# Gated delta-rule layer with feed-forward block: the keys decayed to the chunk's end are turned by way of DRAM and VectorE instead of on TensorE

## What is computed

```python
def step(carry, inp):
    S, R = carry
    q_t, k_t, v_t, a_t, aR_t, b_t, g_t = inp
    kn = k_t / jnp.maximum(jnp.linalg.norm(k_t, axis=-1, keepdims=True), 1e-12)
    pred = jnp.einsum('bhji,bhj->bhi', S, kn)
    r = jnp.clip(v_t - pred, -CLIP, CLIP)
    S = a_t[..., None] * S
    kp = jnp.einsum('bhd,bhde->bhe', kn, S)
    S = S + b_t[..., None, None] * kn[..., None] * (v_t - kp)[..., None, :]
    o = jnp.einsum('bhji,bhj->bhi', S, q_t)
    R = aR_t[..., None] * R
    kpR = jnp.einsum('bhd,bhde->bhe', kn, R)
    R = R + g_t[..., None, None] * kn[..., None] * (r - kpR)[..., None, :]
    o = o + jnp.einsum('bhji,bhj->bhi', R, q_t)
    return ((S, R), o)
```

## Time and profile before

| what | value |
|---|---|
| median of 2 runs | 2404.26 us (2404.12 to 2404.41) |
| profiled execution, device time | 2413.72 us |
| its span, first to last instruction | 2411.9 us, mean granted TensorE clock 0.973 |
| TensorE matmuls, weight loads | 2283.6 us (95%), 1927.4 us (80%) |
| VectorE, ScalarE, GpSimd | 1686.8 us (70%), 1240.2 us (51%), 1169.0 us (48%) |
| `turn_kend` (L433) on the chain that ended last | 4% of the span |

### The profile page before, as it was taken

The page is one execution under the profiler, slowest core; times in us unless marked ns, Lnnn a source line. Parts: engine busy times, 40 slices in busy tenths (PEclk is TensorE's granted clock), DMA queues, the critical chain, the costliest instruction groups (busy, mean ns, idle before and its releaser), DMA issues.

```text
span 2411.9 us, 120326 instructions
## 1 busy us (share of the span) xinstructions
PE 2283.6 (95%) x52544; PEld 1927.4 (80%) x52544; DVE 1686.8 (70%) x3725; ACT 1240.2 (51%) x2384; POOL 1169.0 (48%) x2376
## 2 busy tenths in 40 slices
PE   1999996699999999999999999999999999999998
PEld 1544443588999888989888888888888988888887
DVE  6111012778888878888888888888888888888874
ACT  2322232555555555555555555555555555555530
POOL 0000000655666665665565666566665666656641
PEclk8899997789999999999999999999999999999998
DMA  3000000111212121212111212112112122222221
GB/s 89 1 0 0 0 0 20 27 37 37 39 37 42 38 47 36 40 38 40 38 38 38 47 38 40 38 38 38 38 38 49 38 40 42 41 43 41 44 42 25
DMA packets 306094, 84.82 MB, mean 35 GB/s; under 512 B 280368, under 2 KB 302512, under 8 KB 305584
## 3 DMA queue, kind: packets, MB, share of 16 engines
q1 hardware_dynamic: 305584, 77.25, 16.1%
HBM read 41.53 MB, written 35.65 MB: 32 GB/s over the span
## 4 chain that ended last, share of the span: by engine, by line
PE 77%; issue 15%; DMA 2%; DVE 2%; POOL 2%; ACT 1%; SPq 1%; POOLq 0%; ACTq 0%; DVEq 0%
PE bank L453 12%; PE bank L476 5%; PE bank L467 5%; PE bank L433 4%; PE bank L497 3%; PE bank L488 3%; PE bank L415 3%; PE bank L410 3%; PE bank L404 3%; PE bank L553 3%; PE bank L612 3%; PE bank L422 3%; PE bank L395 3%; PE bank L530 3%; PE bank L521 2%
## 5 line engine op out<-in xcount | busy, mean ns | idle before, releaser
L1069 POOL TENSOR_TENSOR lane_t<-lane_n,lane_x 128x15 f32<-128x15 f32 (+7 forms) x960 | 317.6, 331 | 375.7 <-DMA lane_n<-n_dram 305.5
L453 PE MATMUL bank<-kq,Kt 64*64 64x96 f32 x8192 | 363.2, 232 | 1.5 <-issue 0.6
L1072 POOL TENSOR_TENSOR lane_x<-lane_x,lane_t 128x15 f32<-128x15 f32 (+7 forms) x960 | 326.5, 340 | 75.2
L453 PEld LDWEIGHTS bank<-kq,Kt 64*64 64x64 f32 x8192 | 316.8, 135 | 3.5 <-issue 3.4
L1228 ACT ACTIVATE oS<-bank 128x512 f32<-128x512 f32 x64 | 38.2, 597 | 351.4 <-PE bank L601 351.4
L1043 POOL TENSOR_TENSOR KQF<-efull,kn 128x768 f32<-128x768 f32 x64 | 124.6, 1946 | 190.9 <-ACT efull L1183 190.9
L1152 ACT ACTIVATE ea<-bank,nba 128x256 f32<-128x256 f32 x256 | 107.3, 470 | 195.2 <-PE bank L415 140.1
L1205 ACT ACTIVATE kend<-Kt,ek 128x64 f32<-128x64 f32 x768 | 189.8, 340 | 0.0
L1086 POOL MEMSET lane_id<- 128x256 f32 x1 | 0.3, 311 | 389.2 <-DVE acc L758 389.2
L755 DVE TENSOR_TENSOR dn<-bank,s3b 128x512 f32<-128x512 f32 x8 | 5.5, 692 | 239.5 <-PE bank L378 239.5
L849 DVE COPY_PREDICATED AS<-cst,bank 128x384 f32<-128x384 int32 x256 | 143.0, 584 | 31.3 <-PE bank L453 28.6
(11 more groups left out here) (156 smaller groups left out, 6490.9 us busy)
## 6 DMA issues: line engine op xcount, KB each, us to landing
XF<-x_dram SPq DMA_DIRECT2D x256, 64.0 KB, 2.4
lane_n<-n_dram SPq DMA_DIRECT2D x128, 124.0 KB, 2.8
x_dram<-lane_x SPq DMA_DIRECT2D x128, 124.0 KB, 2.3
n_dram<-AS SPq DMA_DIRECT2D x256, 32.0 KB, 2.0
n_dram<-AR SPq DMA_DIRECT2D x256, 32.0 KB, 1.7
wt<-in_win SPq DMA_DIRECT2D x4, 640.0 KB, 4.7
out_y<-acc SPq DMA_DIRECT2D x16, 128.0 KB, 2.0
hw<-in_h1T SPq DMA_DIRECT2D x1, 1024.0 KB, 7.3
```

The costliest lines, as they stand in the source:

```text
L453: ins = pe.matmul(v3(dst[hd[h], o:o + kinds * C], kinds)[:, :, i * SUB:(i + 1) * SUB], Kt[hd[h], m * 96 + i * SUB:m * 96 + i * SUB + C], r ...
L1069: pool.tensor_tensor(tv, lane_n[:, m * SUB + m + 1:m * SUB + BASE].unsqueeze(2).to_broadcast([L, rows, m + 1]), xv[:, m, 0:m + 1].unsqueez ...
L1072: pool.tensor_tensor(xv[:, m + 1:, 0:m + 1], xv[:, m + 1:, 0:m + 1], tv, ALU.subtract).then_inc(s["lane_step"], 1)
```

## The change

`turn_kend` and `copy_kend` are removed, with their semaphores. SyncE writes `kend` to a new DRAM buffer `k_dram` (one DMA of 128 x 3072 bytes) and reads it back into a new SBUF tile `kend_in` with four DMAs of 32 partitions (two runs of 1536 bytes each a partition), so that the halves of the tokens and of the head dimension have changed places between the partition blocks. VectorE then transposes all blocks of 32 x 32 in one instruction of 128 x 768 into `kendT[n % 2]` (two buffers in place of three). `to_end` writes `kend` in the matching order: halves of the tokens outermost. SyncE's new DMAs stand between `lanes_in` and `lanes_out` of the same quad; VectorE's transpose of quad k stands first in its body k. `project_kq` no longer waits for the copy, and `to_end` waits for the DMA out of `kend` instead of for the turning.

```diff
@@ -182,7 +182,8 @@
             KQF = ring("KQF", RING, 5 * 2 * (T - C))
             dec = ring("dec", RING, NM)
             vt = ring("vt", RING, 2 * T)
-            kendT = ring("kendT", 3, 4 * (T - C))
+            kend_in = sbb("kend_in", 4 * (T - C))
+            kendT = ring("kendT", 2, 4 * (T - C))
             AS = ring("AS", 3, NCH * 2 * 3 * C)
             AR = ring("AR", 3, NCH * 2 * 2 * C)
 
@@ -205,6 +206,7 @@
             rS = ring("rS", 2, P)
             oS = sbb("oS", 2 * T)
 
+        k_dram = nc.dram_tensor("k_dram", (2, 4, SUB, 4 * (T - C)), F32).ap()
         n_dram = nc.dram_tensor("n_dram", (2, 4, NM, SUB, SUB), F32).ap()
         x_dram = nc.dram_tensor("x_dram", (2, 4, NM, SUB, SUB), F32).ap()
 
@@ -299,6 +301,20 @@
                     sp.dma_start(lane_n[j * half_lanes:(j + 1) * half_lanes, 0:LANE_RUN],
                                  n_dram[n % 2].rearrange("e m s t -> (e m) (s t)")[:, run]).then_inc(s["n_in"], 16)
 
+            def keys_out(n):
+                need(sp, "kend", n + 1)
+                need(sp, "k_in", (n - 1) * 4 * 16)
+                sp.dma_start(k_dram[n % 2].rearrange("e d t -> (e d) t"), kend[:, :]).then_inc(s["k_out"], 16)
+
+            def keys_in(n):
+                need(sp, "k_out", (n + 1) * 16)
+                need(sp, "kT", n)
+                for h in range(2):
+                    for j in range(2):
+                        e = 2 * h + j
+                        sp.dma_start(v3(kend_in[e * SUB:(e + 1) * SUB, :], 2),
+                                     k_dram[n % 2, 2 * h:2 * h + 2, :, j * 2 * (T - C):(j + 1) * 2 * (T - C)].rearrange("i d t -> d i t")).then_inc(s["k_in"], 16)
+
             def store(n):
                 b = n % B
                 need(sp, "acc_add", n + 1)
@@ -310,6 +326,8 @@
                     blocks_out(k + 2, 0)
                     blocks_out(k + 2, 1)
                     lanes_in(k + 2)
+                    keys_out(k + 2)
+                    keys_in(k + 2)
                     lanes_out(k + 2)
                 if on(k + 5) and (k + 5) % B == 0:
                     load_weights(k + 5)
@@ -388,7 +406,6 @@
 
             def project_kq(n):
                 need(pe, "w_loaded", (n // B + 1) * 16)
-                need(pe, "kT_sb", 2 * (n - 1))
                 need(pe, "kn", n)
                 need(pe, "vt_sb", n)
                 for p in range(2):
@@ -422,17 +439,6 @@
                         ins = pe.matmul(PA1[hd[h], c * P:(c + 1) * P], xh(n)[:, c * C:(c + 1) * C], wt[:, 4 * 256 + h * P:4 * 256 + (h + 1) * P],
                                         start=True, stop=True)
                 ins.then_inc(s["v_ps"], 1)
-
-            def turn_kend(n):
-                need(pe, "kend", n + 1)
-                need(pe, "kn", min(n + 2, NQ))
-                need(pe, "vt_sb", min(n + 2, NQ))
-                for y in range(2):
-                    for m in range(6):
-                        for h in range(2):
-                            ins = pe.matmul((PA0, PA1)[y][hd[h], m * DH:(m + 1) * DH], kend[hd[h], (y * 6 + m) * C:(y * 6 + m + 1) * C],
-                                            ident[hd[h], hd[h]], start=True, stop=True)
-                    ins.then_inc(s["kT_ps"], 1)
 
             def products(n, g):
                 y, chunks = (0, (g,)) if g < NCH else (1, (2 * (g - NCH), 2 * (g - NCH) + 1))
@@ -523,11 +529,11 @@
 
             def s_s(n, c):
                 need(pe, "sy_sb", 4 * n + c + 1)
-                need(pe, "kT_sb", 2 * n + 2)
+                need(pe, "kT", n + 1)
                 for p in range(2):
                     for h in range(2):
                         o = (p * 3 + c) * C
-                        ins = pe.matmul(SB[hd[h], 2 * P + p * DH:2 * P + (p + 1) * DH], kendT[n % 3][hd[h], o:o + C], pc(yS[c % 2], p)[hd[h], :],
+                        ins = pe.matmul(SB[hd[h], 2 * P + p * DH:2 * P + (p + 1) * DH], kendT[n % 2][hd[h], o:o + C], pc(yS[c % 2], p)[hd[h], :],
                                         start=True, stop=True)
                 ins.then_inc(s["ss_ps"], 1)
 
@@ -581,11 +587,11 @@
 
             def r_s(n, c):
                 need(pe, "ry_sb", 4 * n + c + 1)
-                need(pe, "kT_sb", 2 * n + 2)
+                need(pe, "kT", n + 1)
                 for p in range(2):
                     for h in range(2):
                         o = (6 + p * 3 + c) * C
-                        ins = pe.matmul(RB[hd[h], 2 * P + p * DH:2 * P + (p + 1) * DH], kendT[n % 3][hd[h], o:o + C], pc(yR[c % 2], p)[hd[h], :],
+                        ins = pe.matmul(RB[hd[h], 2 * P + p * DH:2 * P + (p + 1) * DH], kendT[n % 2][hd[h], o:o + C], pc(yR[c % 2], p)[hd[h], :],
                                         start=True, stop=True)
                 ins.then_inc(s["rs_ps"], 1)
 
@@ -618,8 +624,6 @@
                 if e:
                     s_p(k - 1, 1)
                     r_s(k - 1, 0)
-                if l:
-                    turn_kend(k + 1)
                 if e:
                     s_w(k - 1, 2)
                     r_w(k - 1, 1)
@@ -871,6 +875,11 @@
                 mask = cst[:, M_Z1:M_Z1 + SUB].bitcast(I32).unsqueeze(1).to_broadcast([P, NM, SUB])
                 dve.copy_predicated(v3(Zf[n % 2][:, :], NM)[:, :, SUB:], mask, v3(IV[:, :], NM)).then_inc(s["z1"], 1)
 
+            def turn_keys(n):
+                need(dve, "k_in", (n + 1) * 4 * 16)
+                need(dve, "rs_ps", 3 * (n - 1))
+                dve.transpose(v4(kendT[n % 2][:, :], 12, 2).rearrange("p m i d -> p i m d"), v4(kend_in[:, :], 2, 12)).then_inc(s["kT"], 1)
+
             def s_right(n, c):
                 need(dve, "sw_ps", 3 * n + c)
                 dve.tensor_tensor(wS[c % 2][:, :], vt[n % RING][:, c * P:(c + 1) * P], SB[:, 0:P], ALU.subtract).then_inc(s["sw_sb"], 1)
@@ -930,6 +939,8 @@
 
             def body(k):
                 a, b, l, d, e, f = on(k + 3), on(k + 2), on(k + 1), on(k), on(k - 1), on(k - 2)
+                if d:
+                    turn_keys(k)
                 if f:
                     s_clip(k - 2, 3)
                 if e:
@@ -1198,19 +1209,13 @@
             def to_end(n):
                 need(act, "kdiag", n + 1)
                 need(act, "kfar", n + 1)
-                need(act, "kT_ps", 2 * n)
+                need(act, "k_out", n * 16)
                 for m in range(4):
                     for c in range(3):
                         o = (m * NCH + c) * 96 + SUB
-                        ins = act.activation(kend[:, (m * 3 + c) * C:(m * 3 + c + 1) * C], Kt[:, o:o + C], ACT.Copy,
+                        ins = act.activation(v4(kend[:, :], 2, 12)[:, :, m * 3 + c], v3(Kt[:, o:o + C], 2), ACT.Copy,
                                              scale=ek[:, 6 * T + m * NCH + c:6 * T + m * NCH + c + 1])
                 ins.then_inc(s["kend"], 1)
-
-            def copy_kend(n):
-                need(act, "rs_ps", 3 * (n - 2))
-                for y in range(2):
-                    need(act, "kT_ps", 2 * n + y + 1)
-                    act.activation(kendT[n % 3][:, y * 2 * (T - C):(y + 1) * 2 * (T - C)], (PA0, PA1)[y][:, 0:2 * (T - C)], ACT.Copy).then_inc(s["kT_sb"], 1)
 
             def level0(n):
                 need(act, "nx0", n + 1)
@@ -1246,8 +1251,6 @@
                 if b:
                     from_anchor(k + 2)
                     gate_inverse(k + 2)
-                if l:
-                    copy_kend(k + 1)
                 if b:
                     to_anchor(k + 2)
                 if a:
```

More of the change, by code:

```diff
@@ L72 @@
     "kk": "k's operands", "kp": "k's operands of the predictions", "qq": "q's operands", "kf": "k against the state", "ea1": "one over S's gate", "kfull": "operands against the state",
-    "kend": "k decayed to the chunk's end", "kT_ps": "turned in PSUM (2)", "kT_sb": "turned in SBUF (2)",
+    "kend": "k decayed to the chunk's end", "k_out": "it is in DRAM", "k_in": "back with its halves of tokens on partitions (4 DMAs)", "kT": "turned",
     "pr_ps": "products in PSUM (6 a quad)", "pr_sb": "masked in SBUF (6 a quad)", "n_sb": "N times beta or gamma (2 a quad)",
```

## The result

The changed kernel took 2441.01 us, median of two runs (2437.09 and 2444.93), against 2404.26: the ratio is 1.0138, 95% interval 1.0074 to 1.0202. Timed again in more rounds it gave 1.0126 of before, interval 1.0104 to 1.0148. So it is slower by a little over 1%, where 1% faster was forecast. Its profiled execution lasted 2444.93 us, span 2443.1.

A forecast was written before the change was run, and what follows sets the result against it. TensorE was taken to set the pace, about 30 us a quad. 0.60 less 0.27 us over 64 quads gave 21 us, plus 3 of pauses: 2380 us against 2404.3, own range 2360 to 2400, stretched to 2352 to 2406.

The forecast's parts named there:

- What goes: TensorE's `turn_kend` block: 24 matmuls and 1.45 us a quad removed, 93 us in all, plus 5.6 us of pauses.
- What `s_w` waits for then: TensorE after `r_s`: `s_w` waits for VectorE's second clip, so 0.60 us a quad is saved, not 1.45.
- The handoff read from the drain: VectorE's clip to TensorE's `s_w` in the last quads, which have no turning: 0.10 us.
- the Trainium skill's rule of the most-contended engine: Relieve the highest-occupancy engine, TensorE, first; as a rival, the block saved whole: 93 us, 2311 us, 10%.
- What VectorE gains: `turn_keys` at the head of VectorE's body: 968 ns transpose, delaying `s_y(k, 0)` 0.27 us a quad, bounds 0.00 and 0.53.
- The way through DRAM: SyncE's store and four loads of the keys: 7.4 us trip, 3.4 us to spare, no cost.
- Rival 2: Keys come back late, VectorE's transpose waits for the loads at its body's head: 13.7 us trip, 2569 us, 6%.
- ScalarE: `copy_kend` leaves a half-idle engine and `to_end` writes two runs: both costed at nothing, `to_anchor` coming earlier.
- The sum: Whole kernel: 0.33 us a quad gained, 21 us, plus 3 us of pauses, 24 us in all.
- pauses that I had counted at 3: TensorE's 5.6 us of unexplained waits before the turning's matmuls, half of them counted as gained.
- The term of 0.33 us: Net gain a quad: 0.60 at `s_w` less 0.27 for VectorE's transpose; 21 us over 64 quads.
- The one with a longer transpose: Rival: VectorE's transpose costs twice the forecast, stall 1.24 us, net loss 0.64 a quad, 2445 us, 8%.

The follow-up runs named there:

- e4: Kernel before without `turn_kend`, ScalarE's `copy_kend` left in (state updates use wrong keys); ratio 0.9842 to the kernel before.
- e7: Changed kernel with `far_half` waiting for `operands_q` and `turn_keys` moved from the head of VectorE's body to before `s_right(3)`; 2365.6 us, ratio 0.9837.
- e8: Changed kernel with `far_half` waiting for `operands_q`, without the five DMAs of the keys and their waits, VectorE turning zeros; 2393.2 us, ratio 0.9955.
- e2: Kernel before with one swap in ScalarE's program, `to_anchor` ahead of `copy_kend`; ratio 1.0112.
- e1: Changed kernel with one added wait: GpSimd's `far_half` starts only when VectorE's `operands_q` of the same quad is done; 2389.0 us, ratio 0.9899.
- e5: Changed kernel with two idle ScalarE activations of 128x384 where `copy_kend` stood, no wait between engines added; 2389.2 us, ratio 0.9934.
- e12: Changed kernel with GpSimd's `far_half` product replaced by a memset, far keys left out of the result; ratio 0.994, one run.
- e11: Changed kernel, `far_half` behind `operands_q`, later transpose, both key projection matmuls ahead of `s_w(2)`, `operands_q` behind `s_solved(2)` and `r_solved(1)`; 2360.4 us, ratio 0.9827.

## Why the prediction was wrong, step by step

- **What goes: right.** 1.45 us a quad left TensorE.
- **What `s_w` waits for then: right.** Forecast 1.17 us from `r_s` to `s_w`, measured 1.18. TensorE after, with the clip (L904) and `s_w` (L513) 0.10 us behind it:

```profile
1520.56 0.40 PE L594 MATMUL bank<-yR,kendT 64*64 64x64 f32 x8
1521.74 0.45 PE L513 MATMUL bank<-Sst,KQF 64*64 64x64 f32 x8 [0.78 <-issue]
...
1521.35 0.29 DVE L904 TENSOR_SCALAR rS<-bank 128x128 f32<-128x128 f32 x1
```

The handoff read from the drain held in the loop. That a block on the busiest engine is worth its full length, which is what the prediction drew from the Trainium skill's rule of the most-contended engine and which gave 93 us, fails here: e4 shows 35 us for the same removal (0.9842).

- **What VectorE gains: right in size, a little short.** The transpose took 0.965 us (forecast 0.968) with the new pattern. It delayed `s_y(k, 0)` by 0.27 us, as worked out. The 0.13 us behind it (`s_s(0)` above all) I had let end in VectorE's idle time; e7 shows that they belong to it. VectorE and TensorE at the head, after:

```profile
1539.22 0.44 DVE L920 SCALAR_TENSOR_TENSOR Rst<-Rst,dec,bank 128x64 f32<-128x64 f32 x2
1539.59 0.97 DVE L881 STREAM_TRANSPOSE kendT<-kend_in 128x768 f32<-128x768 f32 x1
...
1540.99 0.72 DVE L876 COPY_PREDICATED Zf<-cst,bank 128x512 f32<-128x512 int32 x1
...
1540.87 0.83 PE L459 MATMUL bank<-kq,Kt 64*64 64x96 f32 x16
1541.81 0.50 PE L527 MATMUL bank<-vt,Zf 64*64 64x64 f32 x8
```

- **The way through DRAM: right.** SyncE after:

```profile
1557.72 1.11 SPq L301 DMA_DIRECT2D lane_n<-n_dram  x2
1558.93 0.53 SPq L307 DMA_DIRECT2D k_dram<-kend  x1
1562.71 1.72 SPq L315 DMA_DIRECT2D kend_in<-k_dram  x4
1573.91 1.11 SPq L276 DMA_DIRECT2D x_dram<-lane_x  x2
...
k_dram<-kend SPq DMA_DIRECT2D x64, 384.0 KB, 3.4
kend_in<-k_dram SPq DMA_DIRECT2D x256, 96.0 KB, 2.2
```

The loads are issued 3.8 us after the store, the last about 1.3 after the first, and land 2.2 later: 7.3 us, forecast 7.4. The transpose waited for them once in 64 quads (3.2 us, in the drain, at 2396 us). Rival 2 didn't happen, and e8 shows that nothing is hidden in the trip.

- **ScalarE: this is the step that failed.** I wrote that `copy_kend` and `to_end` cost nothing, since "what follows on ScalarE (`to_anchor` above all) comes earlier rather than later". It did come earlier, and I took earlier for harmless. But `to_anchor` releases GpSimd's `far_half`, which before the change followed `operands_q` by 0.6 us and now starts 0.15 ahead of it; and VectorE, which gets there sooner since `r_s` to `s_w` is shorter, comes to `scale_blocks` 0.55 us closer behind GpSimd's product. (That this second part comes from the turning and not from the copies is shown by e2 and e4: with the turning left in, `scale_blocks` takes 0.76 us at the median, with the copies left in 1.30.) The price on VectorE's way to `s_solved(2)` is 1.10 us on `operands_q` in 58 of 60 quads and 0.55 to 0.63 on `scale_blocks` in more than half. How much of it TensorE sees is read from e1: with `scale_blocks` held `s_s(2)` starts 0.13 us behind the end of `s_solved` (1704.76, 1704.63), of which 0.10 is the handoff, so VectorE's room there is 0.6 to 0.7 us. The delay of `scale_blocks` alone fits in (e1: 1.92 us in nearly all quads, held or not). That of `operands_q` alone comes out at 1.10 - 0.65 = 0.45, and the quads after with `scale_blocks` at 0.68 us show 2.32 (+0.40). Both give 1.73 - 0.65 = 1.08, and the quads with 1.30 us show 2.94 (+1.02). e1, e5 and e12, each by another means, bring `operands_q` back to 1.21 to 1.25 us and the quad to 29.55 to 29.59. The term that I left out was worth 0.92 us a quad at the median, against a sum of 0.33.
- **The sum.** e1 is the change with this term gone: 2389.0 against 2413.6 us, 24.6 us gained where I had forecast 24. That it fits so well is luck in good part. Its sum of medians is 0.17 us shorter and not 0.33, and what the mean lies above it is 0.30 a quad in place of 0.45: together 0.32 x 64 = 20 us, half of it from pauses that I had counted at 3. The rest lies outside the steady loop. And e5 and e12, with the same quad, gained only 16.1 and 15.0 us, since the kernel before was 8.4 and 7.4 us faster in their rounds. The term of 0.33 us was itself about twice too large: the turning gave back 0.57 and not 0.60 (e4), and the transpose at the head cost 0.40 and not 0.27, which leaves 0.17.
- **Rivals.** None of the three was it. The one with a longer transpose ended at 2445 us, near the measured 2441, but by chance: it put 1.84 us on the transpose, which took 0.97 as forecast, where 1.10 and some 0.6 fell on `operands_q` and `scale_blocks`.

## What to carry to other kernels

Work that looks idle, here 0.9 us of copies on a half-idle engine, can be what keeps two other engines from meeting; when it goes, list for every instruction that now starts earlier which engines it releases and what they will run beside. Look above all at pairs of a VectorE instruction with two SBUF inputs and a GpSimd instruction that reads SBUF, and keep the one on the critical path first, with a wait if need be (here one line took the ratio from 1.0126 to 0.9899). And an engine that is busy 99% of the time is worth relieving only as far as the next thing that it waits for, which is read off the other engines' timelines before any matmul is removed. The waits have to be read again after each gain, over the whole loop: in e11 a load that comes three times in 64 quads took back 15 us of the 41 that 64 shorter quads had given.

## What the runs showed of the hardware that I had not expected

- A VectorE product of two SBUF tensors (128x1024) took 2.31 us instead of 1.21 when GpSimd's product of two SBUF tensors had started 0.15 us ahead, and the product of 512 columns 1.31 instead of 0.68 with 0.24 of lead: VectorE ended a fixed time (1.08 and 0.55 us) behind the end of GpSimd's instruction; a GpSimd memset in its place cost it nothing, and a GpSimd copy issued 0.29 us behind it took 1.18 us instead of 0.39.
- TensorE's pauses without a shown cause are not a fixed sum. The wait for the clip at `s_w` set apart, they come to 15.7 us in the loop before (30 pauses), 10.3 after, 7.0 in e1, 3.0 in e7 and 2.1 in e11. What makes them wasn't tried.
- VectorE's transpose in blocks of 32 costs the same with strided runs of 32 on the output: 965 ns for 768 columns, on the line between the 704 and 1230 of the earlier trace rows.
